# Scores of two attention units in alternate PSUM banks, and three steps of the first layer's batch body in another order

## The reference

```python
sim = einsum('bhid,bjd->bhij', q, k) + bias      # (first layer: q and k normalised, times 8)
sim = where(causal, neg, sim); sim = where(mask, sim, neg)
out = einsum('bhij,bjd->bhid', softmax(sim), v)
return layernorm(out @ Wout)
```

## Time and profile before

| | |
|---|---|
| median of 3 runs | 617.21 us |
| profiled execution: its time | 615.22 us |
| profiled execution: span from first to last instruction | 613.5 us |
| mean granted TensorE clock | 0.931 |
| PE busy | 494.4 us (81%) |
| DVE busy | 434.3 us (71%) |
| ACT busy | 378.3 us (62%) |
| POOL busy | 308.8 us (50%) |
| first layer's attention, bodies | about 25 to 220 us |
| second layer's attention, bodies | about 300 to 475 us |

### The profile page before, as it was taken

How to read it: one execution, slowest core, us unless ns; L and a number is a source line. 1 busy time by engine, 2 the same in 40 slices (tenths; PEclk the granted TensorE clock), 3 DMA queues, 4 the chain that set the end, 5 groups by cost and what they waited for, 6 DMA issues and landing times.

```text
span 613.5 us, 13848 instructions
## 1 busy us (share of the span) xinstructions
PE 494.4 (81%) x3220; PEld 397.3 (65%) x3220; DVE 434.3 (71%) x2147; ACT 378.3 (62%) x1475; POOL 308.8 (50%) x367
## 2 busy tenths in 40 slices
PE   2688999999999878958799999988786609999940
PEld 1366777777776655738688787777665507788730
DVE  3989989999998885562768888899888522434313
ACT  1478888788888845733787887877776003434420
POOL 4567756655565617554234234334764540546660
PEclk9769999999999998987799999999999858999985
DMA  6340017422000000000012111000111021232117
GB/s 195 75 155 19 20 33 149 107 75 75 4 5 9 6 1 1 1 1 6 5 44 75 39 45 37 5 9 6 34 34 30 33 68 40 59 79 64 52 34 209
DMA packets 54692, 29.70 MB, mean 48 GB/s; under 512 B 19884, under 2 KB 51572, under 8 KB 54644
## 3 DMA queue, kind: packets, MB, share of 16 engines
q1 hardware_dynamic: 48900, 22.09, 14.5%
q0 software_dynamic: 2560, 4.90, 2.5%
q10 hardware_dynamic: 3184, 2.16, 1.2%
HBM read 16.13 MB, written 10.90 MB: 44 GB/s over the span
## 4 chain that ended last, share of the span: by engine, by line
PE 44%; DVE 23%; issue 14%; ACT 5%; DMA 5%; SPq 3%; POOL 3%; DVEq 1%; another core or an unknown queue 1%; ACTq 0%; POOLq 0%
PE psS L850 7%; PE psS L1147 6%; DVE sc L1539 6%; PE psQ L823 5%; PE psO L886 3%; PE psA L905 3%; PE psQ L1137 3%; PE psQ L807 2%; DVE centred L1602 2%; DVE OT L1563 2%; PE psQ L1071 2%; PE psT L868 2%; DVE qss L1519 1%; PE psO L1137 1%; DVE qn L1530 1%
## 5 line engine op out<-in xcount | busy, mean ns | idle before, releaser
L1248 ACT ACTIVATE sc<-sc,negmax 128x97 f32<-128x97 f32 (+3 forms) x512 | 178.9, 353 | 34.4 <-DVE negmax L1539 34.2
L850 PE MATMUL psS<-kk,qT 128*128 128x194 f32 (+3 forms) x512 | 105.2, 328 | 25.7 <-DVE negmax L1539 23.8
L1539 DVE CUSTOM_DVE_ANT_0 sc<-psS,wide_buf 128x97 f32<-128x97 f32 (+3 forms) x512 | 93.3, 237 | 30.5 <-PE psS L850 24.5
L628 POOL TENSOR_TENSOR wide_buf<-bias,mask 128x132 f32<-128x132 f32 (+3 forms) x128 | 108.4, 873 | 9.8 <-DVE negmax L1539 4.2
L850 PEld LDWEIGHTS psS<-kk,qT 128*128 128x128 f32 x512 | 79.4, 195 | 52.1 <-issue 49.0
L1248 ACT ACTIVATION_READ_ACCUMULATOR sc<-sc,negmax 128x1 f32 x512 | 97.1, 190 | 0.0
L576 POOL TENSOR_TENSOR qrn<-qssc,half 128x9 f32<-128x9 f32 (+1 forms) x32 | 55.6, 1738 | 63.7 <-DVE qssc L1525 63.7
L1551 DVE TENSOR_TENSOR pn<-sc,rsum 128x128 f32<-128x128 f32 (+3 forms) x128 | 74.4, 581 | 8.0 <-DVE rsum L1547 0.3
L905 PE MATMUL psA<-Wo,OT 128*128 128x128 f32 (+1 forms) x512 | 65.7, 283 | 1.7 <-DVE OT L1563 1.7
L905 PEld LDWEIGHTS psA<-Wo,OT 128*128 128x128 f32 x512 | 62.7, 196 | 2.7 <-DVE OT L1563 2.5
L1563 DVE TENSOR_SCALAR OT<-psO,cols 128x512 f32<-128x512 f32 x64 | 47.6, 744 | 3.5 <-PE psO L886 1.8
(11 more groups left out here) (298 smaller groups left out, 1003.5 us busy)
## 6 DMA issues: line engine op xcount, KB each, us to landing
slot_rows<-empty SPq DMA_DIRECT2D x2, 1390.0 KB, 10.0
xb<-slot_rows SPq DMA_DIRECT2D x16, 139.0 KB
vp_u<-vp SPq DMA_DIRECT2D x128, 8.0 KB, 1.7
choice_rows<-zero_row SPq DMA_DIRECT2D x8, 256.0 KB, 3.0
wide_buf<-choice_rows SPq DMA_DIRECT2D x8, 256.0 KB, 5.1
vp_u<-vp SPq DMA_DIRECT2D x64, 16.0 KB, 1.8
eW<-in_L_ffn_W SPq DMA_DIRECT2D x4, 256.0 KB, 3.1
gT<-in_L_ffn_W SPq DMA_DIRECT2D x4, 256.0 KB, 3.0
```

The costliest lines, as they stand in the source:

```text
L628: pool.tensor_tensor(unit_masked(i, u).rearrange("p h e k -> p (h e) k"), unit_bias(layer, u).rearrange("p h e k -> p (h e) k"), mask[laye ...
L850: m = pe.matmul(psS[:, h, 0:2 * w], qT[i][:, h, u].rearrange("p m q -> p (m q)"), kk[i][:, :, 0:w], start=True, stop=True)
L1248: m = act.activation(v, v, ACT.Exp, bias=negmax[:, u, g:g + 1], scale=-1.0, accum_out=psum_row[:, u, g:g + 1])
L1539: dve.tensor_tensor_reduce(sc[u][:, h, e, :], unit_psum(u)[:, h, e, :], unit_masked(i, u)[:, h, e, :], -1.0, -FAR, ALU.add, ALU.min, accum ...
```

## The change

It does three things.

1. **Banks.** `score_bank` gives both halves of units 0, 1 and 2 the same bank, `u % 2`, side by side (units 0 and 2 in bank 0, unit 1 in bank 1). Unit 3 is too wide for that: its half 0 goes to bank 1, its half 1 to bank 0. PE's waits follow: unit 0 waits until unit 3 of the entry before is read, unit 1 too (and so no longer for unit 0), unit 2 until unit 0 is read, half 0 of unit 3 until unit 1 is read, and half 1 of unit 3, behind a wait of its own, until unit 2 is read. This holds in both layers.
2. **PE's order in the first layer.** Scores 1 go ahead of the second `project_heads`, and scores 2 ahead of `project`.
3. **DVE's order in the first layer.** `out_stats`, `moments` and `out_centred` leave their three places in the body (ahead of `qssc`, behind `biased` 2, and behind `kd`) and follow one another at its end, behind `divide(b, 1)`.

```diff
-        def unit_psum(u):
-            return psS[:, :, 0:2 * WIDTH[u]].rearrange("p h (e k) -> p h e k", e=2)
+        def score_bank(u, h):
+
+            w = WIDTH[u]
+            if u == UNITS - 1:
+                return psS[:, 1 - h, 0:2 * w]
+            return psS[:, u % 2, 2 * w * h:2 * w * (h + 1)]
...
-                      (s["scores_ready"], 4 * n))
+                      (s["scores_ready"], 4 * (n - u) if u < 2 else 4 * (n - 1)))
                 for h in range(2):
-                    m = pe.matmul(psS[:, h, 0:2 * w], qT[i][:, h, u].rearrange("p m q -> p (m q)"),
+                    if u == UNITS - 1 and h == 1:
+                        apart(pe, (s["scores_ready"], 4 * n))
+                    m = pe.matmul(score_bank(u, h), qT[i][:, h, u].rearrange("p m q -> p (m q)"),
                                   kk[i][:, :, 0:w], start=True, stop=True)
...
                     scores(0, b, 0, i)
                     if not first:
                         values_pair(b - 1, 1 - i)
+                    scores(0, b, 1, i)
                     if not last:
                         project_heads(b + 1, 1, 1 - i)
-                    scores(0, b, 1, i)
...
                         turn_probs(b - 1, 3, 1 - i)
+                    scores(0, b, 2, i)
...
                         project(0, b - 2, i, not last)
-                    scores(0, b, 2, i)
                     if not first:
                         values(b - 1, 1 - i)
                     scores(0, b, 3, i)
...
-                    dve.tensor_tensor_reduce(sc[u][:, h, e, :], unit_psum(u)[:, h, e, :], unit_masked(i, u)[:, h, e, :],
+                    dve.tensor_tensor_reduce(sc[u][:, h, e, :], score_bank(u, h)[:, e * WIDTH[u]:(e + 1) * WIDTH[u]],
+                                             unit_masked(i, u)[:, h, e, :],
...
-                    if reads:
-                        out_stats(0, b - 2, i)
                     if not last:
                         floored(b + 1, 1)
                     biased(n + 2, 2, i)
-                    if reads:
-                        moments(b - 2, i)
                     if not last:
                         keys_in(b + 1, 1 - i)
                     else:
                         dense_stats(1)
+                    divide(b, 1)
                     if reads:
+                        out_stats(0, b - 2, i)
+                        moments(b - 2, i)
                         out_centred(b - 2, i)
-                    divide(b, 1)
```

## The result

The changed kernel takes **627.10 us**, the median of 4 runs (626.62 to 629.09), beside 617.31 us for the kernel before in 4 runs on the same chip. The ratio is 1.0164, with a 95% interval of 1.014 to 1.0187: slower by 9.8 us. The profiled execution took 626.62 us, with a span of 624.9 us at a mean granted clock of 0.941.

A forecast was written before the change was run, and what follows sets the result against it. The prediction took a first-layer loop from PE's transposes through ACT to DVE as the bound. Thirteen bodies' +6.4, body 1's -0.5 and body 15's +0.4 made +6.3 us: 621.5 us profiled, 623.5 against the median; range 617.0 to 629.0.

The forecast's parts named there:

- the side that had the chance of 0.68: Whole kernel: slower by over 0.5%; within 0.5% had 0.20, faster 0.12.
- The loop in the place named: First layer: `biased` 2, scores 3, `turn_input`, `turn_keys`, `xnT`, `qss`, next `biased` 2; later `Y` adds 0.49 us a body.
- The signs: First layer: bodies 12.2 to 12.5 us, PE idle some 0.5 behind `Y`, `xnT` wait about 1.4, `qss` waiting every body.
- Release of `turn_input`: First layer: from the end of DVE's `Y` to the PE step it releases, 0.25 us.
- the slot of `o_st`: First layer, `qss` to next `biased` 2: moving `o_st` out saves 0.20 us, 5.99 becoming 5.79.
- the idling ahead of `biased` 2: First layer, DVE: 0.15 us of idling may go or be register-wait cost; half taken, 0.07 us saved.
- The last: First layer, body 15: no transposes behind it, DVE's chain alone counts, +0.4 us.
- 0.5 forecast for body 1: First layer, body 1, with no `Y` to wait for: unit 3's first-half scores run earlier, -0.5 us.
- I count 0: Second layer: earlier scores 2 gain nothing, since `values` still waits for `OT` until 361.45; 0 us.
- The bare waits cost nothing: First layer rival, chance 0.17: `y_done` 0.38 us earlier, loop 11.99 us; +0.9 in all, 618.1 us, no change.
- The scores' waits were the bound: Rival, chance 0.11: second layer's scores 2 give back 5.6 us, first layer loses nothing; 611.6 us.
- The collision of `divide` with POOL: First layer rival, chance 0.06: unit 2's later `divide` meets POOL's bias additions, 2.9 us atop the high end; 631.7 us.

The follow-up runs named there:

- experiment 4, dve_back: The whole change with DVE's old order: 613.79 us, ratio 0.9958.
- banks_only: The kernel before with the new score banks and their waits, both orders old: 612.03 us, ratio 0.9932.
- y_late: The kernel before with `out_centred` alone moved behind `divide(b, 1)`: 618.75 us, ratio 1.0063.
- woven: The whole change with DVE's last steps ordered `biased` 2, `out_stats`, `kd`, `moments`, `out_centred`, `divide`: 616.23 us, ratio 1.0022.
- keys_fill, experiment 6: The whole change with `kd` moved ahead of `floored(b + 1, 1)`, between `qss` and `qssc`: 623.00 us, ratio 1.0122.
- dve_only: The kernel before with the new DVE order alone, old banks and old PE order: 629.79 us, ratio 1.0191.
- keys_first: The new banks alone (both orders old), with `turn_input` and `turn_keys` ahead of scores 3 on PE: 617.02 us, ratio 1.0036.
- mask_late, experiment 9: The new banks alone, with POOL's first-layer bias addition of unit 2 moved behind `q_rsqrt(b + 1, 0)`: 621.83 us, ratio 1.0086.
- experiment 11: The new banks alone, with POOL's first-layer bias addition of unit 2 kept in place but waiting for unit 2's `divide`: 613.02 us, ratio 0.9916.

## Why the prediction was right, and where it was off

**The direction and the mechanism held.** 627.10 us lies in the range of 617.0 to 629.0, on the side that had the chance of 0.68. The loop in the place named is what grew: `turn_input` waits for `Y`, `xnT` for the transposes, `qss` for `qsq` in every body. Experiments 2 and 4 show it from both sides: the DVE order alone gives 12.83 us a body, its removal 11.86. The signs came, but larger than forecast: bodies of 12.83 us for 12.2 to 12.5, PE idle 1.10 us ahead of `turn_input` for 0.5, ACT's wait ahead of `xnT` 1.74 us for 1.4.

One sum carries all of it. From `xnT` to `qss` it is 3.25 us and from `qss` to the next `biased` 2 5.99 us, in the earlier trace rows and in nearly every variant, so the body is as long as the start of `xnT` behind `biased` 2, plus 9.24:

| kernel | `xnT` behind `biased` 2 | plus 9.24 | body measured |
|---|---|---|---|
| before, a shorter body | 2.46 | 11.70 | 11.70 |
| banks_only, a shorter body | 2.38 | 11.62 | 11.61 |
| dve_back | 2.38 | 11.62 | 11.86 |
| y_late | 2.85 | 12.09 | 12.09 |
| woven | 2.84 | 12.08 | 12.08 |
| keys_fill | 3.32 | 12.56 | 12.57 |
| dve_only | 3.59 | 12.83 | 12.83 |
| the change | 3.59 | 12.83 | 12.83 |

Where it does not hold, another wait sits in one of the two legs: in dve_back `o_st` waits for `project`, in keys_first `qT` comes late, in mask_late `pn` of unit 0 takes 0.74 us longer (12.36 against 11.62), and in bodies 5, 7, 9 and 11 of before and of banks_only `pn` of unit 2 meets POOL's addition. The prediction's 11.88 us is a mean over both kinds of body; the loop that it describes is that of the 11.70.

**The size was off**: 12.37 us forecast, 12.83 measured, 0.46 us a body. By terms:

- `biased` 2 to `kd` 0.72, `rsum` to `pn` 0.20, `pn` 0.34, `o_st` to `moments` 0.40: as forecast. Of the two lengths of `pn` the choice of the shorter was right.
- `moments` to `Y`: 0.28 forecast from code written out, 0.40 measured in the loop (and 0.28 again in body 3, written out). `kd` to `rsum` was 0.27 for 0.30. Together +0.09.
- Release of `turn_input`: 0.30 for 0.25 (0.10 in body 3); to `turn_keys` 0.14 for 0.11; to `xnT` 0.47 for 0.45. Together +0.10.
- **The largest miss: "the slot of `o_st` (0.20, 143.63 to 143.83) leaves it, so 5.79".** It stayed 5.99. In the kernel before, `o_st` stood between `qss` and `qssc`, which waits for `qss`:

```profile
143.03 0.68 DVE L1519 TENSOR_REDUCE qss<-qsq 128x8 f32<-128x512 f32 x1
143.83 0.16 DVE L1525 TENSOR_SCALAR qssc<-qss 128x8 f32<-128x8 f32 x1
```

That pair is 0.80 us apart with `o_st` between them and 0.78 without (136.61 to 137.39 above). The step had filled a wait, and its leaving gave back 0.02 us instead of 0.20. Experiment 6 shows the same with `kd`. The 0.07 us granted for the idling ahead of `biased` 2 did not come either: 0.16 us stand there still, now put down to "issue" and not to PE. Together +0.27.

The number of bodies was nearly right, 12 in place of 13, but each paid 0.94 us and not 0.49. The last cost 0.1 us for the forecast 0.4, and the first two together brought 0.4 of the 0.5 forecast for body 1.

**The second layer's "I count 0" was wrong**, on the other side. For its steady bodies the argument holds. The row of `values` waiting for `OT` is there, as the earlier trace rows had it, and the scores' wait has turned into it; both of the changed kernel, waits of 305 to 480 us:

```profile
PE psO L892 <- DVE OT L1570: 11.0, 11, 1.6
PE psS L856 <- DVE negmax L1545: 4.8, 2, 2.5
```

In the steady bodies the banks alone took 11.30 us for 11.33. But I had read one steady body for sixteen. In the banks alone body 0, where the scores follow each other without work between them, took 1.2 us less, and the last six 0.9. The 0.9 lies in one body, the one from 12 to 13 (11.54 us for 12.49), and experiment 2, with the old banks, has 11.40 us there: it is not shown to be the banks'. From body 0 to 15 the ten profiles with the new banks show 173.7 to 175.4 us, the three without 175.5 to 176.3. Why the ten differ among themselves, with the same code in that layer's bodies, was not settled. So the layer as a whole is shorter with the new banks, by 1.3 us in the mean, and the rest of their 5.1 us has no place shown. The stretch between the layers was not read ahead of the prediction at all.

So the errors partly offset each other. DVE's order by itself cost 12.65 us (experiment 2) where my terms made 6.8 (the 6.3 with the -0.5 of the scores taken out): 5.85 too low. Of the banks' gain of 5.11 us 0.5 was forecast, so 4.61 was missed, and PE's order, +1.76, was counted at nothing. 6.3 + 5.85 - 4.61 + 1.76 is 9.3. That the measured time stayed within the range is in part luck: with DVE's order alone it is 629.79 us, above the upper end of 629.0, and the gain of the banks that I had not seen brought it back.

**The rivals.** "The bare waits cost nothing" fell: its body was 11.99 us, and the measured one takes 12.83. Between y_late (12.09) and dve_only (12.83) stand 0.74 us, of which the two bare waits are 0.51: `o_st` 0.40 for 0.20 to the next step, `moments` 0.40 for 0.09. Most of the rest is the place of `o_st` itself, 0.20. "The scores' waits were the bound" fell in the first layer. In the second the new banks do gain, though not by the mechanism named there: `values` still waits for `OT`. The collision of `divide` with POOL did not add to the change: `pn` of unit 2 takes 0.66 us in the body shown, in a body that idles 0.88 us ahead of `qss`.

## What to carry to other kernels

Before a step is moved, ask what it was filling: a DVE step between a reduction and its reader cost 0.01 to 0.02 us here, where the same `kd` took 0.27 us of the chain behind `biased` 2, and steps that need each other cost most when they are put together at the end of a chain. Look at who waits for the last of them: here one semaphore guard on a shared PSUM bank made the output's normalization part of the loop that feeds the next body. And where a wait is written off because another stands behind it in one body, read the first, the last and the unusual bodies as well. A gap read in code written out can be longer in a hardware loop (0.28 and 0.40 us here for the same pair), so take it from the loop that it is used for.

## What the runs showed of the hardware

**Dependent steps on DVE.** A reader of the step just ahead starts later than an independent step does: behind a statistic of 0.29 us after 0.40 instead of 0.20, behind a reduction of 0.68 us after 0.78 (136.61 to 137.39), where an independent `kd` started after 0.59 (136.60 to 137.19) in experiment 6. The Trainium skill, "VectorE: DVE Perf Modes", section "The DRAIN you can't avoid", has eight copies taking the same time with a semaphore behind each. These rows do not agree with taking that for steps that read one another: here 0.2 us stands between the two cases. In this kernel every such reader also has a semaphore wait, so no run separates the wait from the dependence.

**DVE and POOL.** `pn` of unit 2, a multiplication of two SBUF operands, takes 0.56 us alone and 1.22 when POOL's bias addition is at work, and `pn` of unit 0 0.29 and 1.03. Made to wait for `pn`, the addition starts 0.17 us behind its end and `pn` keeps its 0.56 us (experiment 11). The Trainium skill, "SBUF — State Buffer", section "Who interferes with whom", says that a DVE instruction with two SBUF inputs contends with a GpSimd instruction that reads SBUF, that the shared ports are an exclusive lock, and that issue order decides who blocks. The trace agrees, from both sides, in the banks alone: where POOL's additions start first they take 2.09 us and `pn` 1.22 (121.84 and 123.13), and where `pn` of unit 2 starts ahead of POOL's third addition `pn` keeps its 0.56 us and the three additions take 2.45 (133.90 and 135.03). Experiment 9 shows the practical side: moving one of the two moves the collision.
